# Interaction-network tower on one core: outer sums as float32 products in two row halves, features spread through DRAM, layer-1 rows turned in their own bank

## The chip, the cores and the metric

One core of one Trainium2 chip runs the kernel. The metric is device time in microseconds for one execution, as the median of several. The engines are TensorE (PE: matmuls, and PEld for its weight loads), VectorE (DVE), ScalarE (ACT), GpSimd (POOL, which here only issues gathers) and SyncE (SP, which issues the other DMAs). SBUF is the memory of 128 partitions on which all engines work. PSUM, eight banks of 512 float32 columns in each partition, is where matmuls put their results. A semaphore wait holds up everything behind it on its engine.

## The reference, cut to what matters

512 rows, each with 39 features of 16 numbers looked up in 39 tables, go through two layers of a compressed interaction network and then through an ordinary three-layer perceptron:

```python
B, M0, D = 512, 39, 16
e = stack([tbl_f[ids[:, f]] for f in range(39)], axis=1)        # [B, 39, 16]
X0 = Xi = e
for W in (W0, W1):                                              # [39*39, 128], [39*128, 128]
    z = einsum('bmd,bnd->bdmn', X0, Xi).reshape(B, D, -1)
    Xi = einsum('bdp,po->bod', z, W)                            # [B, 128, 16]
    res.append(Xi)
z = sum(concatenate(res, axis=1), axis=-1)                      # [B, 256]
h = concatenate([z, dense_ctx], axis=1)                         # [B, 272]
h = relu(h @ W_top1 + b_top1); h = relu(h @ W_top2 + b_top2); y = h @ W_top3
```

The sum over `d` at the end lets the second layer be computed without its own pairwise products: for each row of the batch the kernel forms G = X1 (128 x 16) times X0 (16 x 39), and multiplies G by W1. These G are called the outer sums here.

## The kernel before, in words

**Tiles, chunks, steps.** The batch is cut into 4 tiles of 128 rows, each tile into 4 chunks of 32 rows. A chunk has 512 columns (32 rows times 16 of d). Layer 1 of a chunk takes PT = 7 steps: in each one, 128 products of feature pairs (DVE, L738) are multiplied with a piece of W0 and summed in a bank. So there are 16 chunks, STEPS = 112 steps and SPT = 28 steps in a tile. Every engine has the same loop over the steps `s` written out, with the work of other stages put at fixed offsets: `chunk_at(s, offset)` gives the chunk whose step 0 was `offset` steps ago. Which engine is how far ahead is decided only by the semaphores.

**Layer 1.** For chunk i, PE multiplies the features `xs` with 0/1 matrices `sel`. This gives two factors a and b, which ACT copies to `factors` (L433), and three selections, which stay in `b_bank`. DVE multiplies a factor with a selection into `z` (L738). ACT rounds `z` to `z_hi` (float32r, L537), DVE takes the remainder `z_lo` (L748), and PE, LAG = 5 steps later, adds three float32r matmuls of 512 columns to `l1_bank[i % 2]` (L943 to L945, for the last step of a chunk one, L941). In tile 0 two steps of a chunk do without the split: one float32 matmul on `z` kept whole, L938.

**From layer 1 to the outer sums.** ACT copies the bank to `xi` (L553, step 11 of the chunk). PE turns `xi` in four transposes into `xi_bank` (L952, step 13). ACT rounds it to `xit_hi` (L559, step 13), and DVE takes the remainder `xit_lo` out of the same bank (`rest_xit`, L755, step 15). The other side of the product is `diag`: for eight rows of the batch, 8 x 16 partitions against 8 x 40 columns, nonzero only where both belong to the same row (the 40th column is a one, for the sum over d). It is filled from factor a: PE turns its first 40 rows in four transposes into `turn_bank` (`turn_a`, L908, step 1), ACT rounds (`take_xt`, L440), DVE takes the remainder (`rest_xt`, L762), and SP spreads `xt` over `diag` in eight DMAs (L394) for each chunk, high and low parts together. The outer sums of eight rows are then three float32r matmuls of 320 columns (`g_block`, L967 to L969). Four such blocks stand at steps 17, 19, 21 and 23 of the chunk, and ACT copies each to `g` (L545) before the next may start, since there is one `g_bank`.

**Layer 2** of a tile is 39 float32 products of 128 columns (L982) into `s2_bank`, spread over the steps of the next tile; for the last tile they stand together at the end. The perceptron for the first three tiles runs in the last steps, and for the last tile at the very end.

**Features.** Gathers (POOL) and lookups fill `feat`. ACT and DVE split it into three bf16 parts, in pieces (`groups`, three to a tile), and PE turns the parts of the next tile in two halves (`turn_x`, L878), which ACT copies to `xs` (L422).

**Banks.** `turn_bank` takes in turn the features' first half, factor a and the turned factor. `xi_bank` takes the features' second half, factor b and the turned `xi`. `turn_free` makes PE wait until what stood in the bank has been taken.

**SP** issues, in this order: the inputs, then for each chunk the eight diagonals, and behind those of chunks 0 to 2 one piece of w1 each, behind those of chunk 3 the perceptron's weights.

## Time and profile before

| | |
|---|---|
| time, median of 3 runs | 270.82 us (270.24 to 270.98) |
| span of the profiled execution | 273.8 us |
| PE busy | 236.8 us, 86% |
| PEld busy | 185.0 us, 68% |
| DVE busy | 195.6 us, 71% |
| ACT busy | 172.6 us, 63% |
| POOL busy | 104.8 us, 38% |
| DMA queue of SP | 27736 packets, 9.09 MB |

The span runs from the first to the last instruction of one profiled execution. The profile's table by slices shows the granted TensorE clock; full speed is 2.4 GHz and the other level is 1.2 GHz. Shares of the whole span hide that the stages differ, so the rows below are by stretch. In a row of the timeline the first number is the start, the second the duration of the row (or of several of one kind, merged), and a matmul's duration includes the draining of its results. Idle time stands in brackets with what ended it.

### The profile page before, as it was taken

The numbers are of one execution on the slowest core, as the hardware profiler recorded it, in microseconds if no ns is written. First come the engines' busy times: TensorE is split into PE (matmuls) and PEld (weight loads), VectorE is DVE, ScalarE is ACT, GpSimd is POOL, SyncE is SP. The second block draws the span as 40 slices with busy tenths as digits, with TensorE's granted clock in tenths as the row PEclk, the third lists the DMA queues.
The fourth block names the chain that finished last, engine by engine and source line by source line (L and its number), as shares of the span: only waits on it lengthen the run. The fifth ranks groups of instructions, "written<-read, shape, count | busy, mean of one in ns | idle before, by whom it ended". The sixth has DMA issues, their size and how long they took to land.

```text
span 273.8 us, 5185 instructions
## 1 busy us (share of the span) xinstructions
PE 236.8 (86%) x1821; PEld 185.0 (68%) x1821; DVE 195.6 (71%) x341; ACT 172.6 (63%) x339; POOL 104.8 (38%) x102
## 2 busy tenths in 40 slices
PE   4686967896975988787989979988999999999997
PEld 4584954443553655555678768776878788988895
DVE  1453985799994588998978699997889978424001
ACT  4674483267584667776796887869677674457202
POOL 4767876425672565686555548300000000000000
PEclk9959595899996899999999999999999999999999
DMA  6900000006420153412021110201011010010000
GB/s 162 229 11 7 6 8 7 4 15 150 93 61 5 25 141 101 101 13 27 8 35 32 28 23 12 29 2 24 11 15 21 12 19 10 16 24 0 2 0 0
DMA packets 30897, 10.21 MB, mean 37 GB/s; under 512 B 21032, under 2 KB 30269, under 8 KB 30872
## 3 DMA queue, kind: packets, MB, share of 16 engines
q1 hardware_dynamic: 27736, 9.09, 15.2%
q0 software_dynamic: 3136, 0.81, 3.3%
q8 instruction: 14, 0.23, 0.3%
q14 instruction: 11, 0.09, 0.1%
HBM read 7.26 MB, written 0.00 MB: 27 GB/s over the span
## 4 chain that ended last, share of the span: by engine, by line
PE 67%; DVE 10%; issue 10%; ACT 8%; another core or an unknown queue 3%; DMA 1%; DVEq 0%; SPq 0%; ACTq 0%
PE s_bank L982 12%; PE l_bank L945 6%; PE l_bank L943 5%; PE l_bank L944 5%; DVE z L738 4%; PE g_bank L967 3%; PE g_bank L968 3%; PE g_bank L969 3%; PE l_bank L857 3%; PE b_bank L857 3%; DVE z_lo L748 2%; PE b_bank L923 2%; PE xi_bank L952 2%; ACT z_hi L537 2%
## 5 line engine op out<-in xcount | busy, mean ns | idle before, releaser
L363 POOL DMA_INDIRECT feat<-tbl,ids_sb x98 | 104.6, 1068 | 68.8 <-PE l_bank L945 30.6
L738 DVE TENSOR_TENSOR z<-factors,b_bank 128x512 f32<-128x512 f32 x96 | 65.0, 681 | 11.4 <-PE l_bank L938 4.0
L537 ACT ACTIVATE z_hi<-z 128x512 fp32r<-128x512 f32 x104 | 65.8, 633 | 11.0 <-DVE z L738 7.6
L748 DVE TENSOR_TENSOR z_lo<-z,z_hi 128x512 fp32r<-128x512 f32 x88 | 60.3, 685 | 3.6 <-ACT z_hi L537 2.7
L982 PE MATMUL s_bank<-g,w_sb 128*128 128x128 f32 x312 | 46.1, 277 | 0.0
L982 PEld LDWEIGHTS s_bank<-g,w_sb 128*128 128x128 f32 x312 | 41.8, 190 | 1.8 <-issue 0.7
L545 ACT ACTIVATE g<-g_bank 128x320 f32<-128x320 f32 x64 | 27.9, 435 | 23.7 <-PE g_bank L969 15.8
L943 PE MATMUL l_bank<-z_hi,w_hi 128*128 128x512 f32 x88 | 42.6, 484 | 0.0
L967 PE MATMUL g_bank<-diag,xit_hi 128*128 128x320 f32 x64 | 28.5, 446 | 8.5 <-issue 5.8
L945 PE MATMUL l_bank<-z_hi,w_lo 128*128 128x512 f32 x88 | 35.0, 397 | 0.0
L944 PE MATMUL l_bank<-z_lo,w_hi 128*128 128x512 f32 x88 | 34.8, 395 | 0.0
L967 PEld LDWEIGHTS g_bank<-diag,xit_hi 128*128 128x128 f32 x64 | 12.7, 199 | 15.6 <-issue 10.7
L923 PE MATMUL b_bank<-xs,sel 117*128 117x512 bf16 x48 | 18.9, 394 | 2.3 <-DVE z L738 1.1
L968 PE MATMUL g_bank<-diag,xit_hi 128*128 128x320 f32 x64 | 20.0, 312 | 0.0
L969 PE MATMUL g_bank<-diag,xit_lo 128*128 128x320 f32 x64 | 19.9, 310 | 0.0
L945 PEld LDWEIGHTS l_bank<-z_hi,w_lo 128*128 128x128 f32 x88 | 16.7, 189 | 3.8
L943 PEld LDWEIGHTS l_bank<-z_hi,w_hi 128*128 128x128 f32 x88 | 17.0, 193 | 1.2 <-issue 0.7
L944 PEld LDWEIGHTS l_bank<-z_lo,w_hi 128*128 128x128 f32 x88 | 16.9, 192 | 0.4
L923 PEld LDWEIGHTS b_bank<-xs,sel 117*128 117x128 bf16 x48 | 4.7, 98 | 15.7 <-issue 9.0
L553 ACT ACTIVATE xi<-l_bank 128x512 f32<-128x512 f32 x16 | 9.6, 597 | 6.8 <-PE l_bank L941 3.9
L568 ACT ACTIVATE g<-b_bank,bt_sb 128x384 f32<-128x384 f32 (+1 forms) x8 | 3.7, 473 | 15.8 <-PE b_bank L1023 11.0
L968 PEld LDWEIGHTS g_bank<-diag,xit_hi 128*128 128x128 f32 x64 | 12.3, 193 | 1.6 <-issue 0.4
(197 smaller groups left out, 405.6 us busy)
## 6 DMA issues: line engine op xcount, KB each, us to landing
diag<-xt SPq DMA_DIRECT2D x128, 20.0 KB
w_sb<-w SPq DMA_DIRECT2D x3, 832.0 KB
feat<-tbl,ids_sb POOLq DMA_INDIRECT x98
wt_sb<-wt SPq DMA_DIRECT2D x2, 512.0 KB
g<-small SPq DMA_DIRECT2D x1, 770.0 KB
g<-small SPq DMA_DIRECT2D x1, 448.0 KB
w0p<-w_pair SPq DMA_DIRECT2D x1, 448.0 KB
w0m<-w_mirror SPq DMA_DIRECT2D x1, 448.0 KB
```

The costliest lines, as they stand in the source:

```text
L363: nc.gpsimd.indirect_dma_start(feat[:, bt % 2, n * D:(n + 1) * D], None, tables[order[n]], bass.IndirectOffsetOnAxis(ids_sb[:, bt, order[n ...
L537: nc.scalar.activation(z_hi[:, s % RING, :], z[:, at, :], ACT.Copy).then_inc(rounded, 1)
L738: nc.vector.tensor_tensor(target, one, other, ALU.mult).then_inc(product, 1)
L748: nc.vector.tensor_sub(low[rows, s % RING, :], z[rows, SPLITS[s] % Z_RING, :], z_hi[rows, s % RING, :].bitcast(f32)).then_inc(remainder, 1)
L923: nc.tensor.matmul(b_bank[q % B_RING][:], sel[:, j, :], columns(*divmod(i, CPT)), start=True, stop=True).then_inc(selected, 1)
L943: nc.tensor.matmul(bank[:], w0_hi[:, t, :], z_hi[:, t, :], start=u == 0, stop=False)
L944: nc.tensor.matmul(bank[:], w0_hi[:, t, :], z_lo[:, t, :], start=False, stop=False)
L945: nc.tensor.matmul(bank[:], w0_lo[:, t, :], z_hi[:, t, :], start=False, stop=False).then_inc(l1_used, 1)
L967: nc.tensor.matmul(o, y_hi, x_hi, start=True, stop=False)
L968: nc.tensor.matmul(o, y_hi, x_lo, start=False, stop=False)
L969: nc.tensor.matmul(o, y_lo, x_hi, start=False, stop=True).then_inc(g_summed, 1)
L982: last = nc.tensor.matmul(s2_bank[:, 0:P], w1_sb[:, order[m], :], g[:, bt % 2, m, :], start=m == 0, stop=m == F - 1)
```

## The change

**Outer sums.** A block is no longer three float32r matmuls but one product in float32, with no rounding and no remainder. Eight rows of the batch are cut in two halves of four (HB = 4): partitions 0 to 63 and 64 to 127 are two matmuls of 64 rows and 160 columns, the upper half into one bank, the lower into another. `g_bank` is now two banks. Two blocks make a group (GS = 2), a chunk has two groups (GPC = 2), at steps 15 and 18, and ACT copies both banks of a group in one instruction. The order of the batch's rows in `g` differs for it, and `dense_ctx` and `y` are permuted to match.

**Layer-1 rows.** `xi` is turned into `l1_bank[i % 2]`, the bank that it came from, and ACT copies it whole (`take_xit`); `rest_xit` is gone. Layer 1 of chunk i waits for the copy of chunk i - 2.

**Diagonals.** `turn_a`, `take_xt` and `rest_xt` are gone. ACT copies each piece of the features, as float32 and ordered by d, to `line` (`keep_line`). Once per tile SP writes `line` to a DRAM scratch `lines`, waits for it, and reads it back in eight DMAs of 16 x 16 runs of 160 bytes into `diag`, which now holds a whole tile. The loop of SP is paced by layer 1 (`l1_used`).

**Banks.** With `xi_bank` gone, `turn_bank` takes features, factor a and factor b. `w0m` borrows the place of `xit`, and the products kept whole have a tensor of their own.

**Steps.** Layer 2 of a tile starts at step 40 and not 45 of it; for tile 2 it is spread over 16 steps and not 12. The perceptron's first part starts at the same step, 117.

```diff
-G_AT = [TURN_XI + 4 + 2 * r for r in range(CH // P)]
-TURN_A = 1
-REST_XT = TURN_A + 1
+G_AT = [TURN_XI + 2, TURN_XI + 5]
+GPC = len(G_AT)
+GS = SUBS // GPC
+HB = SB // 2
...
+LINE_AT = [[1, 2, 3], [10, 16, 21], [11, 18, 24], [11, 18, 24]]
...
-S2_STEPS = [SPT - 2] * (TILES - 2) + [12]
+S2_STEPS = [SPT - 2] * (TILES - 2) + [16]
...
-        xit_hi = sb("xit_hi", [P, 2, CH], f32r)
-        xit_lo = sb("xit_lo", [P, 2, CH], f32r)
-        xt = sb("xt", [P, 2, 2, SUBS, GW], f32r)
-        diag = sb("diag", [P, 2, 2, SUBS, SB, GW], f32r)
+        xit = sb("xit", [P, 2, CH])
...
+        line = sb("line", [P, 2, D, GW])
+        diag = sb("diag", [P, 2, CPT * SUBS, HB, GW])
...
-        xi_bank = bank("xi_bank")
-        g_bank = bank("g_bank")
+        g_bank = ctx.enter_context(nc.psum_tensor("g_bank", [P, 2, 512], f32))
+        g_banks = [g_bank[:, h, :] for h in range(2)]
...
                 if bt >= 2:
                     pool.wait_ge(*after(turn_filled, "x", bt - 2, XJ - 1))
+                    pool.wait_ge(lined, line_pieces[bt - 1])
...
+            def spread_lines(bt):
+
+                sp.wait_ge(lined, line_pieces[bt + 1])
+                sp.dma_start(lines[bt], line[:, bt % 2, :, :]).then_inc(line_out[bt], 16)
+                sp.wait_ge(line_out[bt], 16)
+                if bt >= 2:
+                    sp.wait_ge(g_summed, CPT * GPC * (bt - 1))
+                for b in range(SB):
+                    sp.dma_start(diag[b * D:(b + 1) * D, bt % 2, :, b % HB, :],
+                                 lines[bt, b::SB].rearrange("r d m -> d r m")).then_inc(diag_in[bt % 2], 16)
...
             for i in range(CHUNKS):
-                sp.wait_ge(*after(turn_taken, "xt", i, 0))
-                if i >= 2:
-                    sp.wait_ge(g_summed, SUBS * (i - 1))
-                for b in range(SB):
-                    sp.dma_start(diag[b * D:(b + 1) * D, i % 2, :, :, b, :].bitcast(f32),
-                                 xt[b * D:(b + 1) * D, i % 2, :, :, :].bitcast(f32)).then_inc(diag_in[i % 2], 16)
+                if i:
+                    sp.wait_ge(l1_used, PT * (i - 1) + 1)
+                if i % CPT == 0:
+                    spread_lines(i // CPT)
...
-            def take_xt(i):
+            def keep_line(bt, k):
+
+                lo, hi = groups[bt][k]
+                if bt >= 2:
+                    act.wait_ge(line_out[bt - 2], 16)
+                act.wait_ge(rest1, split_no[bt, k] + 1)
+                nc.scalar.activation(line[:, bt % 2, :, lo:hi],
+                                     feat[:, bt % 2, lo * D:hi * D].rearrange("p (m d) -> p d m", d=D),
+                                     ACT.Copy).then_inc(lined, 1)
...
-            def round_xit(i):
-                act.wait_ge(*after(turn_filled, "xi", i, 0))
+            def take_xit(i):
+                act.wait_ge(xi_turned, i + 1)
                 if i >= 2:
-                    act.wait_ge(g_summed, SUBS * (i - 1))
-                nc.scalar.activation(xit_hi[:, i % 2, :], xi_bank[:], ACT.Copy).then_inc(xit_hi_done, 1)
+                    act.wait_ge(g_summed, GPC * (i - 1))
+                nc.scalar.activation(xit[:, i % 2, :], l1_bank[i % 2][:], ACT.Copy).then_inc(xit_copied, 1)
...
-            def rest_xit(i):
-            def rest_xt(i):
-            def turn_a(i):
...
             def g_block(j):
...
+                for q in range(GS):
+                    r = n * GS + q
+                    for h in range(2):
+                        rows = slice(h * P // 2, (h + 1) * P // 2)
+                        last = nc.tensor.matmul(g_banks[h][:, q * HB * GW:(q + 1) * HB * GW],
+                                                xit[rows, i % 2, r * P:(r + 1) * P],
+                                                diag[rows, bt % 2, c * SUBS + r, :, :].rearrange("p b m -> p (b m)"),
+                                                start=True, stop=True)
+                last.then_inc(g_summed, 1)
```

On PE, in a chunk of tile 1 (layer 2 of tile 0 runs beside it), from a selection over one block of outer sums to the turn of factor a, this stood before:

```order
L923 MATMUL b_bank0<-xs,sel 128x512 [waits product]
L967 MATMUL g_bank<-diag,xit_hi 128x320 [waits g_copied]
L968 MATMUL g_bank<-diag,xit_hi 128x320
L969 MATMUL g_bank<-diag,xit_lo 128x320
L982 MATMUL s2_bank<-g,w1_sb 128x128
L943 MATMUL l1_bank0<-z_hi,w0_hi 128x512 [waits remainder]
L944 MATMUL l1_bank0<-z_lo,w0_hi 128x512
L945 MATMUL l1_bank0<-z_hi,w0_lo 128x512
L908 MATMUL turn_bank<-id32,factors 128x40 [waits turn_taken0]
L908 MATMUL turn_bank<-id32,factors 128x40 x3
L982 MATMUL s2_bank<-g,w1_sb 128x128 x2
```

and this now, at the first group of a chunk:

```order
L914 MATMUL b_bank0<-xs,sel 128x512 [waits product]
L978 MATMUL s2_bank<-g,w1_sb 128x128 x2
L934 MATMUL l1_bank0<-z_hi,w0_hi 128x512 [waits remainder]
L935 MATMUL l1_bank0<-z_lo,w0_hi 128x512
L936 MATMUL l1_bank0<-z_hi,w0_lo 128x512
L961 MATMUL g_bank<-diag,xit 128x160 [waits g_copied,xit_copied]
L961 MATMUL g_bank<-diag,xit 128x160 x3
L978 MATMUL s2_bank<-g,w1_sb 128x128
```

Two blocks of three became one group of four, and the turn of factor a (L908) is gone.

On PE, where the features of the next tile are turned in two halves, before (`parts` is what the features were split into; `turn_taken0` is counted when the content of `turn_bank` was taken, `turn_taken1` for `xi_bank`):

```order
L878 MATMUL turn_bank<-id16,parts 117x128 [waits kept,rest2,turn_taken0]
L878 MATMUL turn_bank<-id16,parts 117x128 x7
L967 MATMUL g_bank<-diag,xit_hi 128x320 [waits g_copied]
L968 MATMUL g_bank<-diag,xit_hi 128x320
L969 MATMUL g_bank<-diag,xit_lo 128x320
L982 MATMUL s2_bank<-g,w1_sb 128x128
L943 MATMUL l1_bank0<-z_hi,w0_hi 128x512 [waits remainder]
L944 MATMUL l1_bank0<-z_lo,w0_hi 128x512
L945 MATMUL l1_bank0<-z_hi,w0_lo 128x512
L878 MATMUL xi_bank<-id16,parts 117x128 [waits turn_taken1]
L878 MATMUL xi_bank<-id16,parts 117x128 x7
```

and now:

```order
L879 MATMUL turn_bank<-id16,parts 117x128 [waits kept,rest2,turn_taken0]
L879 MATMUL turn_bank<-id16,parts 117x128 x7
L978 MATMUL s2_bank<-g,w1_sb 128x128 x2
L934 MATMUL l1_bank0<-z_hi,w0_hi 128x512 [waits remainder]
L935 MATMUL l1_bank0<-z_lo,w0_hi 128x512
L936 MATMUL l1_bank0<-z_hi,w0_lo 128x512
L879 MATMUL turn_bank<-id16,parts 117x128 [waits turn_taken0]
L879 MATMUL turn_bank<-id16,parts 117x128 x7
```

The second half waits for the copy of the first, with no outer sums between them.

On DVE, around the last step of a chunk in tile 1, before:

```order
L738 TENSOR_TENSOR z<-factors,b_bank1 128x512 [waits turn_taken1,selected,rounded,remainder]
L748 TENSOR_TENSOR z_hi<-z,z_hi 39x512 [waits l1_used,rounded]
L755 TENSOR_TENSOR xit_lo<-xi_bank,xit_hi 128x512 [waits g_summed,xit_hi_done]
L646 TENSOR_TENSOR rest<-feat 128x128 [waits kept,rest2,gathered2_2]
L738 TENSOR_TENSOR z<-factors,b_bank0 128x512 [waits selected,rounded,remainder]
L748 TENSOR_TENSOR z_lo<-z,z_hi 128x512 [waits l1_used,rounded]
L762 TENSOR_TENSOR xt<-turn_bank,xt 128x4x39 [waits diag_in1,xt_hi_done]
L653 TENSOR_TENSOR parts<-rest 128x16x8 [waits turn_filled1,rest1]
```

and now:

```order
L756 TENSOR_TENSOR z<-factors,b_bank1 128x512 [waits turn_taken0,selected,rounded,remainder]
L766 TENSOR_TENSOR z_hi<-z,z_hi 39x512 [waits l1_used,rounded]
L667 TENSOR_TENSOR rest<-feat 128x128 [waits kept,rest2,gathered2_2]
L756 TENSOR_TENSOR z<-factors,b_bank0 128x512 [waits selected,rounded,remainder]
L766 TENSOR_TENSOR z_lo<-z,z_hi 128x512 [waits l1_used,rounded]
L674 TENSOR_TENSOR parts<-rest 128x16x8 [waits turn_filled0,rest1]
```

The two remainders L755 and L762 are gone; the rest stands in the same order.

## Rows read from the trace of the kernel before

**Rows 1.** Windows by stage: from:to, us, then busy us of PE, PEld, DVE, ACT, POOL; clock.

```profile
54.00:76.00 22.00, 18.57 (x77) 9.44 (x77) 21.58 (x39) 14.07 (x28) 10.23 (x11) 1.00 0.41 90
76.00:95.00 19.00, 14.49 (x68) 9.56 (x67) 12.14 (x23) 11.72 (x24) 9.92 (x11) 0.82 0.12 18
95.00:128.00 33.00, 27.57 (x137) 18.74 (x137) 30.15 (x53) 23.83 (x52) 21.95 (x21) 1.00 0.36 81
128.00:156.00 28.00, 25.61 (x165) 20.38 (x164) 22.79 (x39) 21.30 (x44) 15.72 (x16) 1.00 0.16 25
156.00:184.00 28.00, 25.62 (x157) 20.07 (x156) 27.20 (x51) 22.28 (x48) 12.08 (x12) 1.00 0.12 16
184.00:258.00 74.00, 72.38 (x445) 60.62 (x443) 51.00 (x87) 48.97 (x99) 0.00 (x0) 1.00 0.09 14
```

**Rows 2.** Windows 54:76, 95:128, 156:184, summed: L755 alone, then L762 alone.

```profile
sum 83.00, DVE 4.84; mean DVE 1.61
...
sum 83.00, DVE 2.83; mean DVE 0.94
```

**Rows 3.** Timeline of DVE: start, duration, engine, line, operation.

```profile
194.17 0.32 DVE L762 TENSOR_TENSOR xt<-turn_bank,xt 128x156 fp32r<-128x156 f32 x1 [0.72 <-ACT xt L440]
194.41 0.68 DVE L738 TENSOR_TENSOR z<-factors,b_bank 128x512 f32<-128x512 f32 x1
195.00 0.69 DVE L748 TENSOR_TENSOR z_lo<-z,z_hi 128x512 fp32r<-128x512 f32 x1
```

**Rows 4.** Timeline of PE, one block of outer sums and what follows it.

```profile
196.56 0.31 PE L967 MATMUL g_bank<-diag,xit_hi 128*128 128x320 f32 x1
...
197.00 0.27 PE L982 MATMUL s_bank<-g,w_sb 128*128 128x128 f32 x1
```

**Rows 5.** Windows with L967 alone: PE busy and count, one for each block.

```profile
128.00:156.00 28.00, 4.09 (x9) 1.77 (x9) 1.00 0.16 25
184.00:258.00 74.00, 11.42 (x28) 5.42 (x28) 1.00 0.09 14
```

**Rows 6.** Windows with L908 alone: PE busy and count, four for each turn.

```profile
128.00:156.00 28.00, 0.88 (x8) 0.64 (x8) 1.00 0.16 25
184.00:258.00 74.00, 1.75 (x16) 1.29 (x16) 1.00 0.09 14
```

**Rows 7.** Timeline of PE around one turn of factor a (L908).

```profile
193.03 0.40 PE L945 MATMUL l_bank<-z_hi,w_lo 128*128 128x512 f32 x1
193.36 0.44 PE L908 MATMUL turn_bank<-id,factors 40*128 40x40 f32 x4
193.73 0.49 PE L982 MATMUL s_bank<-g,w_sb 128*128 128x128 f32 x2
...
194.29 0.39 PE L944 MATMUL l_bank<-z_lo,w_hi 128*128 128x512 f32 x1
194.52 0.40 PE L945 MATMUL l_bank<-z_hi,w_lo 128*128 128x512 f32 x1
```

**Rows 8.** Lines of PE from 258.2 to 266.8: count, busy us, mean ns.

```profile
L982 PE MATMUL s_bank<-g,w_sb 128*128 128x128 f32 x78 | 9.0, 276 | 0.0
```

**Rows 9.** Timeline of PE, the two turns of tile 3's features.

```profile
182.37 0.63 PE L878 MATMUL turn_bank<-id,parts 128*117 128x128 bf16 x8 [0.72 <-DVE parts L653]
...
184.25 0.44 PE L878 MATMUL xi_bank<-id,parts 128*117 128x128 bf16 x5
```

**Rows 10.** Timeline of ACT, the copy of the first half.

```profile
183.86 1.02 ACT L422 ACTIVATE xs<-turn_bank 117x1024 bf16<-117x1024 bf16 x1
```

**Rows 11.** Timeline of SP: the first chunk's eight diagonals, issue time.

```profile
57.60 5.24 SPq L394 DMA_DIRECT2D diag<-xt  x8
```

**Rows 12.** Timeline of PE, the first block of outer sums of the program.

```profile
73.58 0.41 PE L967 MATMUL g_bank<-diag,xit_hi 128*128 128x320 f32 x1
```

**Rows 13.** Waits: who waited, releaser, total us, times, longest us.

```profile
ACT g L545 <- remote: 6.0, 3, 2.9
```

**Rows 14.** DMA issues: KB, us from issue to landing.

```profile
ids_sb<-ids SPq DMA_DIRECT2D x1, 78.0 KB, 1.9
```

More of the change, by code:

```diff
@@ L284, in build @@
         chunk0_taken = sem("chunk0_taken")
-        xt_hi_done = sem("xt_hi_done")
+        lined = sem("lined")
+        line_out = [sem(f"line_out{j}") for j in range(TILES)]
         w0_summed = sem("w0_summed")
@@ L318, in build @@
         fills = [[("x", 0, 0)], [("x", 0, 1)], [("a", 0, 0)], [("b", 0, 0)]]
-        for s in range(LAST):
+        for s in range(STEPS):
             bt, v = divmod(s, SPT)
-            if (i := chunk_at(s, TURN_A)) is not None:
-                fills[0].append(("xt", i, 0))
             if bt + 1 < TILES:
@@ L342, in after, with turn_bank_of @@
             return sems[k], n + 1
+        def turn_bank_of(*job):
+            return turn_banks[fill[job][0]]
+        line_pieces = [sum(len(groups[b]) for b in range(t)) for t in range(TILES + 1)]
         MLP_MM = H1T + H2T + 1
@@ L423, in take_x @@
                     xs[:, bt % 2, first:end, k * D // XJ:(k + 1) * D // XJ],
-                    turn_banks[k][0:R, :].bitcast(bf16).rearrange("p (d b) -> p b d", b=P)[:, first:end, :],
-                    ACT.Copy).then_inc(signal or turn_taken[k], 1)
+                    turn_bank_of("x", bt, k)[0:R, :].bitcast(bf16).rearrange("p (d b) -> p b d", b=P)[:, first:end, :],
+                    ACT.Copy).then_inc(signal or turn_taken[fill["x", bt, k][0]], 1)
             def take_factor(name, i):
@@ L588, in _ @@
                             keep_next(bt + 1, k)
+                for t in (bt, bt + 1):
+                    for k, at in enumerate(LINE_AT[t] if t < TILES else ()):
+                        if v == at and (t == 0 or t == bt + 1):
+                            keep_line(t, k)
                 if s == TOP_AT[0]:
@@ L591, in _ @@
                     nc.scalar.activation(wt1_hi[:], wt1_sb[:], ACT.Copy).then_inc(top_rounded, 1)
-                for j, (at, part) in enumerate(zip(ZS_AT, whole)):
+                for j, (at, part) in enumerate(zip(ZS_AT, (z1, z2))):
                     if s == at:
@@ L791, in _ @@
                     rest_z(s - Z_LAG)
-                if (i := chunk_at(s, REST_XI)) is not None:
-                    rest_xit(i)
-                if (i := chunk_at(s, REST_XT)) is not None:
-                    rest_xt(i)
                 if bt + 1 < TILES:
@@ L899, in fill_factor @@
                 k = fill[name, i, 0][0]
-                nc.tensor.matmul(turn_banks[k][:], sel[:, SELECTS + "ab".index(name), :], columns(i // CPT, i % CPT),
+                nc.tensor.matmul(turn_banks[k], sel[:, SELECTS + "ab".index(name), :], columns(i // CPT, i % CPT),
                                  start=True, stop=True).then_inc(turn_filled[k], 1)
-            def turn_a(i):
-                turn_free("xt", i, 0)
-                pe.wait_ge(*after(turn_taken, "a", i, 0))
-                for r in range(SUBS):
-                    last = nc.tensor.transpose(turn_bank[:, r * GW:(r + 1) * GW],
-                                               factors[0:GW, i % F_RING, 0, r * P:(r + 1) * P],
-                                               id32[0:GW, 0:GW])
-                last.then_inc(turn_filled[fill["xt", i, 0][0]], 1)
             def select(i, j):
```

135 lines of the change are left out of this document (57 added, 78 removed).

## The prediction

> **What bounds the kernel now.** Read the table by stretches first [rows 1]. Its columns give, for each stretch, how long each engine was busy. What to look for is which engine fills the stretch. The work stages begin at 54 us, when the first product of tile 0 starts. VectorE (DVE) fills 21.58 of 22 us, then 30.15 of 33 us (95 to 128) and 27.20 of 28 us (156 to 184). TensorE (PE) fills 72.38 of the 74 us from 184 to 258, and in 128 to 156 it is ahead of DVE, 25.61 to 22.79. In 76 to 95 neither is full: that stretch has a halt and a lower granted clock, 0.82 of full. So a microsecond taken from DVE counts in three stretches (83 us), one taken from PE in two others (102 us).
>
> Then read starts, not durations. A row's duration on PE contains the time in which results drain while the next matmul already streams. The float32r product L967 lasts 0.31 us, but its row and the next two start 0.15 us apart, and the row behind the three starts 0.44 us after the first [rows 4]. 0.44 us is what one block of outer sums costs PE. On DVE the rows last 0.68 but start 0.60 apart, and the small L762 takes 0.24 [rows 3].
>
> **Part 1: the remainders leave DVE.** Each chunk loses `rest_xit` (L755, 0.60) and `rest_xt` (L762, 0.24). In the three stretches where DVE is full the sums of their busy time are 4.84 and 2.83 us; divided by 0.69 and 0.31 us a row (0.32 in [rows 3] is one such row) that is 7 and 9 instructions [rows 2]. 7 x 0.60 + 9 x 0.24 = 6.4 us less on DVE. What is late next is PE: it is busy 18.57, 27.57 and 25.62 us there, with draining in it. In the first two it leaves room. In 156 to 184 the gap between DVE and PE is only 1.6 us (27.20 less 25.62) where DVE loses 2.5, so I take 1.5 there. Part 1: 5.4 us gained, between 4.4 (if PE soon catches up in the second too) and 6.4.
>
> **Part 2: the outer sums on PE.** Before: 64 blocks of three float32r matmuls of 320 columns. After: 32 groups, each of two column ranges by two row halves, written as four float32 matmuls of 160 columns. A float32 matmul is issued as two instructions: the program asks for 39 products of layer 2 in a tile, and the last tile shows 78 rows of L982, back to back [rows 8]. 9.0 us for 78, less one drain of 0.16, is 0.114 us for 128 columns; 160 columns cost in proportion 0.14. A group is thus 8 instructions of 0.14.
>
> Two things decide its price. First, the array changes from full height to halves and back for each group. The nearest row is the old turn of the factors (L908, 40 rows, tile of 64): from L945 at 193.03 to L944 at 194.29 is 1.26 us, in which stand L945 (0.23, as L944 to L945 one step on), two L982 (0.11 each) and L943 (0.23); 0.58 is left for four tiny transposes [rows 7]. They start some 0.07 apart (0.44 us busy in all, of which the last is 0.235), so 0.27 is their own and 0.31 is entering and leaving the mode. Second, whether the two halves run at the same time. If they do not, the group is 0.31 + 8 x 0.14 = 1.43 us. If they do, the second instruction of the upper half can run beside the first of the lower one, but a half still runs its own two in order; in this order of issue the eight take five slots: 0.31 + 5 x 0.14 = 1.01 us. No row of before shows two halves at once. I take 1.01, since the halves share neither rows of the array, nor weights, nor a bank (h goes to its own bank), and the turn's rows show that the array does treat a 64-row tile as a mode of its own. Both ends stay for the range.
>
> By the Trainium skill (TensorE: Matmul & The Clock Gate, Part 3: Packing small matmuls), matmuls at different row positions run concurrently, starting about 4 ns apart, while matmuls otherwise stay in program order; with full pairing a group would be 0.31 + 4 x 0.14 = 0.87 us and my sum 2.6 us lower. No run here shows that yet.
>
> In the two stretches that PE fills there are 9 + 28 blocks [rows 5] and 8 + 16 transposes, six turns [rows 6]. Before: 37 x 0.44 + 6 x 0.58 = 19.8 us. After, 18.5 groups: 18.7 us overlapped (1.1 gained), 26.5 us one after another (6.7 lost). So the precision change by itself brings PE little; the removed turns pay for the mode changes.
>
> **Part 3: one bank for five kinds of fills.** The factors a and b and both halves of the features now go through `turn_bank`. Fill a, a step after fill b, waits for ScalarE's (ACT's) copy of b; behind it on PE stand layer 1's matmuls of that step. Where DVE paces, PE has that slack. Where PE paces, a step lasts 1.5 us (L945 to L945 in [rows 7]), and ACT's copy of 512 columns, shorter than the 1.02 us of the features' copy of 1024 [rows 10], fits in it: cost 0. Without that cover (ACT late with its other work) it is up to 0.5 us for each of 12 chunks. The second half of the features has no such room: the first turn starts at 182.37, the second at 184.25 [rows 9], and ACT's copy in between takes 1.02 us [rows 10]. Now the second waits for the end of that copy. With the outer sums no longer between them PE would arrive about 0.4 us early: 0.4 x 3 tiles = 1.2 us lost (0 to 3).
>
> **Part 4: features by way of DRAM.** 128 small transfers become 4 writes and 32 reads, and w1 queues behind 9 of them and not behind 8. ACT trades 16 `take_xt` for 12 `keep_line`, and half of its `take_g` rows for rows of twice the size; it is never the full engine [rows 1], so 0. The first tile alone is tight. The lines are complete after step 3, about 60 us; a write lands in some 2 us (ids_sb took 1.9 [rows 14]); the eight reads are issued in 5.2 us, as the eight diagonals were [rows 11]; they land 2 us later, at 69. The first outer sums stood at 73.58 [rows 12] and now are due two steps sooner, at about 71. Cover 2 us: cost 0, up to 4 if the landing is late. Later tiles have 15 steps of cover.
>
> **Part 5: looser coupling.** `take_g` once in 3 or 4 steps and not in 2, and one copy fewer between turn and outer sum. PE's gaps in the stretches it fills sum to 2.4 + 1.6 us [rows 1]; I take 0.7 of it.
>
> **Sum.** -5.4 - 1.1 + 1.2 + 0 - 0.7 = -6.0 us. The profiled execution has a span of 273.8 us, 3.0 above the median of 270.82; I carry the difference over unscaled: 270.82 - 6.0 = 264.8 us, with 261 to 268 for this case. All bounds here are inside: 4.4 instead of 5.4, 3 instead of 1.2.
>
> **Rivals.**
> A. The halves run one after another. Part 2 becomes +6.7, and in 156 to 184 PE's own growth leaves 1.0 of the 2.5. Part 1 is then 4.9: -4.9 + 6.7 + 1.2 = +3.0, so 273.8 us, slower. It decides at the group's price: above 1.35 us a group (halfway and more to 1.43) the gain of part 1 is eaten. For it: no row shows an overlap, and each float32 product has two ordered instructions. Against it: separate rows, weights and banks.
> B. The first reads land late. The w1 pieces and gathers share the queues with them, and PE waits at the first group: +3 to +4 on the forecast, 268.5 us. For it: 2 us of cover only, two trips in a row. Against it: w1 is now issued behind the reads, where before it went between the first diagonals.
> C. The early halts go. ACT stood three times, 6.0 us in all, before L545, released by nothing that the profile knows [rows 13], and the stretch from 76 to 95 has them and the low clock [rows 1]. If they come from transfers among the w1 pieces, the other order may end some of them: -5 more, 259.5 us. Against it: nothing names their cause.
> That the change does not do what it says is A.
>
> **How the numbers follow.** Forecast 0.50, A 0.20, B 0.15, C 0.15. A is the only case that ends above 271.6; B and the upper edge of the forecast leave some 0.08 within 0.3% (about 0.8 us, what a measurement here can tell from no change). Faster 0.72, same 0.08, slower 0.20. The range 258.0 to 273.5 holds the forecast, B, most of C and the nearer third of A.
>
> **What would show it.** DVE: no rows of L755 and L762, and DVE no longer full in 95 to 128. PE: start to start of the four products of a group, 0.14 within a half, and from the first to the row behind the group, 0.85 (overlapped, less the entry) or 1.25. PE idle before the second turn of a tile's features about 0.4 us. The first outer sum at 71 to 72 us, with diag landed. Wrong would be: a group at 1.4 us or more; PE waiting for ACT's factor copies in every chunk; the first group later than 73.6.

## The result, and the profile after

On the chip of the prediction the changed kernel takes 262.92 us in the median of four runs (260.08 to 266.09), against 270.9 before. The ratio, here and below, leaves out executions more than 1.5% above the fastest of their kernel (here 264.5 and 266.1 us): it is 0.962, with a 95% interval from 0.954 to 0.970. The forecast was 264.8 us, and the range 258.0 to 273.5.

The experiments ran later, on chips with the numbers 0, 2, 8 and 15; the number of the first chip is not recorded. On those four the kernel before takes 252.9 to 253.3 us, and on chip 0, beside the changed kernel, 253.1 against 244.7, a ratio of 0.966 (0.962 to 0.970). Of the 23.0 us between the two profiles of the kernel before (273.8 and 250.8), 13.2 lie ahead of the part that is studied here: the first product stands at 53.9 us on the first chip and at 40.7 us on chip 0. The other 9.8 lie in chunks 0 to 9.

The stages of the changed kernel, as [rows 1], by the same columns. The stretches stand where its own stages stand:

```profile
52.20:76.00 23.80, 17.18 (x76) 9.33 (x76) 22.19 (x38) 17.21 (x33) 10.67 (x12) 1.00 0.60 140
76.00:95.00 19.00, 15.02 (x86) 9.26 (x87) 14.11 (x24) 14.09 (x27) 12.89 (x13) 1.00 0.37 88
95.00:128.00 33.00, 28.62 (x172) 19.33 (x171) 29.69 (x52) 26.29 (x50) 21.96 (x23) 1.00 0.13 18
128.00:156.00 28.00, 25.32 (x168) 18.39 (x166) 23.54 (x40) 23.64 (x41) 17.50 (x18) 1.00 0.17 29
156.00:184.00 28.00, 27.62 (x187) 20.57 (x185) 24.46 (x43) 23.11 (x44) 5.11 (x5) 1.00 0.09 21
184.00:246.00 62.00, 61.22 (x396) 48.02 (x396) 37.83 (x63) 37.00 (x65) 0.00 (x0) 1.00 0.02 4
```

Two things changed against [rows 1]. The stretch 76 to 95 has the full clock (it had 0.82). And in 156 to 184 the full engine is now PE (27.62 of 28 us) and no longer DVE (24.46, it was 27.20). In 95 to 128 DVE is still nearly full, at 29.69 of 33 (it was 30.15), with 22 products of L756 where there were 21 of L738. In 76 to 95 neither engine is full, as before.

One group of outer sums, in the timeline of PE (start, duration, then what ran), with its neighbours:

```profile
191.34 0.39 PE L935 MATMUL l_bank<-z_lo,w_hi 128*128 128x512 f32 x1
191.56 0.40 PE L936 MATMUL l_bank<-z_hi,w_lo 128*128 128x512 f32 x1
191.89 0.81 PE L961 MATMUL g_bank<-diag,xit 64*128 64x160 f32 x8
192.63 0.49 PE L978 MATMUL s_bank<-g,w_sb 128*128 128x128 f32 x2
```

And the same group in very short windows, with L961 alone (the number behind x counts the matmul rows that are running in the window):

```profile
191.88:191.90 0.02, 0.01 (x2) 0.01 (x2) 1.00 0.00 0
...
192.12:192.14 0.02, 0.02 (x4) 0.02 (x4) 1.00 0.00 0
...
192.26:192.28 0.02, 0.02 (x6) 0.02 (x4) 1.00 0.00 0
```

Within 20 ns two rows start, and later two more within 20 ns, and so on: the eight instructions run as four pairs. The starts are 191.890 and 191.896, then 192.13, 192.27 and 192.40, each with a partner 6 ns later. L936 has streamed for its 0.22 us by 191.79; the group starts 0.1 later, its first pair takes 0.24 and the others 0.135, and of the 0.21 between the two L978 behind it 0.1 is more than their usual 0.11. In all a group costs PE 0.95 us: 4 x 0.135 = 0.54, and 0.41 beyond it, which I put down to entering and leaving the mode.

The price of the shared bank, in the list of waits (who waited, for whom; us in total, times, longest us):

```profile
DVE z L756 <- ACT factors L447: 10.7, 8, 2.2
...
PE turn_bank L901 <- ACT factors L447: 7.5, 5, 3.2
```

Before, DVE's wait for the same copy was 3.8 us, six times, and PE had no such wait among its longer ones. The first group, and SP's issues ahead of it:

```profile
70.67 0.81 PE L961 MATMUL g_bank<-diag,xit 64*128 64x160 f32 x8
```

```profile
57.12 0.35 SPq L395 DMA_DIRECT2D lines<-line  x1
59.30 4.04 SPq L400 DMA_DIRECT2D diag<-lines  x8
63.39 5.53 SPq L419 DMA_DIRECT2D w_sb<-w  x3
```

It stands at 70.67 us, 2.9 us earlier than the first block in [rows 12], and PE did not wait for `diag` there. Of the 2.9 us, 1.7 lie ahead of chunk 0, which starts at 52.2 us and not at 53.9.

The halts of [rows 13] are there again, though shorter: where ACT stood 6.0 us in three, the list of waits of the changed kernel on this chip has

```profile
ACT g L564 <- remote: 3.2, 2, 2.5
```

and more of the kind before other copies of ACT.

### The profile page after: what moved, and what is told of

Its sections match the earlier page's. It is cut to its first block, busy times and chain, and to the rows that moved or that the text cites. A ratio compares the mean times of both kernels' runs of the same rounds, so it can differ in the third digit from the quotient of the medians.

```text
span 258.2 us, 4953 instructions
## 1 busy us (share of the span) xinstructions
PE 220.1 (85%) x1821; PEld 163.4 (63%) x1821; DVE 182.5 (71%) x308; ACT 171.8 (67%) x303; POOL 103.1 (40%) x102
## 4 chain that ended last, share of the span: by engine, by line
PE 69%; ACT 10%; issue 9%; DVE 7%; another core or an unknown queue 2%; DMA 1%; SPq 0%; ACTq 0%; DVEq 0%
PE s_bank L978 15%; PE g_bank L961 7%; PE l_bank L936 7%; PE l_bank L934 7%; PE l_bank L935 6%; ACT z_hi L555 3%; PE b_bank L914 3%; PE l_bank L942 2%; PE turn_bank L901 2%; PE g_bank L858 2%; PE s_bank L858 2%; PE turn_bank L879 2%; PE l_bank L858 2%; PE l_bank L1043 2%
## 5 line engine op out<-in xcount | busy, mean ns | idle before, releaser
L368 POOL DMA_INDIRECT feat<-tbl,ids_sb x98 | 102.9, 1050 | 61.2 <-PE l_bank L936 26.3
L756 DVE TENSOR_TENSOR z<-factors,b_bank 128x512 f32<-128x512 f32 x88 | 60.3, 685 | 16.4 <-ACT factors L447 10.7
L555 ACT ACTIVATE z_hi<-z 128x512 fp32r<-128x512 f32 x104 | 63.6, 631 | 7.6 <-PE l_bank L936 2.7
L978 PE MATMUL s_bank<-g,w_sb 128*128 128x128 f32 x312 | 48.5, 282 | 2.4 <-ACT g L564 1.3
L978 PEld LDWEIGHTS s_bank<-g,w_sb 128*128 128x128 f32 x312 | 43.0, 192 | 8.4 <-issue 5.1
L564 ACT ACTIVATE g<-g_bank 128x640 f32<-128x640 f32 x32 | 22.5, 702 | 21.0 <-PE g_bank L961 17.4
L936 PE MATMUL l_bank<-z_hi,w_lo 128*128 128x512 f32 x88 | 34.9, 396 | 0.0
L961 PE MATMUL g_bank<-diag,xit 64*128 64x160 f32 x256 | 26.1, 322 | 3.5 <-ACT xit L578 2.8
L961 PEld LDWEIGHTS g_bank<-diag,xit 64*128 64x128 f32 x256 | 18.3, 186 | 14.9 <-issue 9.3
L447 ACT ACTIVATE factors<-turn_bank 128x512 f32<-128x512 f32 x30 | 17.9, 596 | 6.2 <-PE turn_bank L901 3.5
L936 PEld LDWEIGHTS l_bank<-z_hi,w_lo 128*128 128x128 f32 x88 | 16.5, 188 | 3.7
L901 PE MATMUL turn_bank<-xs,sel 117*128 117x512 bf16 x30 | 11.6, 386 | 7.5 <-ACT factors L447 7.5
L578 ACT ACTIVATE xit<-l_bank 128x512 f32<-128x512 f32 x16 | 9.6, 598 | 3.3 <-remote 3.3
```

The source lines that it names most:

```text
L368: nc.gpsimd.indirect_dma_start(feat[:, bt % 2, n * D:(n + 1) * D], None, tables[order[n]], bass.IndirectOffsetOnAxis(ids_sb[:, bt, order[n ...
L447: nc.scalar.activation(factors[:, i % F_RING, "ab".index(name), :], turn_banks[k], ACT.Copy).then_inc(turn_taken[k], 1)
L555: nc.scalar.activation(z_hi[:, s % RING, :], z[:, at, :], ACT.Copy).then_inc(rounded, 1)
L564: nc.scalar.activation(to.rearrange("p m (k q) -> p m k q", k=2), g_bank[:, :, 0:GS * HB * GW].rearrange("p k (q m) -> p m k q", m=GW), AC ...
L756: nc.vector.tensor_tensor(target, one, other, ALU.mult).then_inc(product, 1)
L936: nc.tensor.matmul(bank[:], w0_lo[:, t, :], z_hi[:, t, :], start=False, stop=False).then_inc(l1_used, 1)
```

## The experiments

Ratios are to the kernel before, in the same comparison on the same chip. Chip 8 had the halves in turn, the products twice and both runs on the remainders; chip 0 the two kernels again and both runs on the fills; chip 2 the later layer 2, the three moves and the bridge; chip 15 the moves and lines. Differences between two kernels are those of their ratios, at 253.1 us, also where the two ran on different chips. The **changed kernel again**, and the **kernel before, profiled again**:

> The changed kernel itself, beside the kernel before on the same chip, since in the last comparison the kernel before took 253.3 us and not 270.8. If the change is worth a fixed share: a ratio of 0.962 to the kernel before. If a part of the gain was the halts and the low clock around 85 us that the kernel before had on the first chip: 0.965 to 0.975. The version with the halves one after another in the program had 0.9655; since both halves ran at once there too, I expect the same here within 0.3%.

Measured: 244.7 us in the median of six, ratio 0.966 (0.962 to 0.970). Four of them lie between 242.6 us, at a mean granted clock of 0.986, and 245.0, at 0.965; the other two took 249.2 and 249.8, at 0.952.

> The kernel before, profiled on this chip. If the halts (all engines idle at about 75, 84 and 115 us) belong to the kernel, they are there again, and the span is that of the table of before. If they belong to the chip or to the one execution, there are none, and the span is some 251 us.

Measured: 252.6 us, span 250.8, and no halt: no wait of ACT before L545 from outside the profile's knowledge, as [rows 13] had, and the clock full from 47 us on. Nor does the list of waits of the next experiment, the changed kernel with another order of the halves, while on the first chip both kernels have them. So the halts come with the first chip or with those executions, and not with the kernel. Since the change is worth the same share, within the intervals, where there are none, they are not where its gain comes from either. What caused them stays open. The profiles on the later chips give a table free of halts; the changed kernel stands in it by the next experiment, whose time is the same. The numbers are spans, in us, between the starts of the first product (L738, L756) of chunks 0, 10 and 15, from the timelines of DVE:

| profile | ahead of chunk 0 | chunks 0 to 9 | 10 to 14 | 15 to the end | span |
|---|---|---|---|---|---|
| kernel before | 40.7 | 102.9 | 55.7 | 51.5 | 250.8 |
| before, without remainders | 40.9 | 98.4 | 54.4 | 51.9 | 245.6 |
| changed (halves in turn) | 41.5 | 99.6 | 54.0 | 47.5 | 242.6 |
| changed, remainders back | 41.2 | 104.7 | 56.7 | 47.5 | 250.1 |
| changed, products twice | 40.9 | 106.3 | 59.5 | 50.3 | 257.0 |
| changed, three moves | 41.1 | 97.2 | 52.2 | 48.4 | 238.8 |

**The order of the halves.**

```diff
-                for q in range(GS):
-                    r = n * GS + q
-                    for h in range(2):
+                for h in range(2):
+                    for q in range(GS):
+                        r = n * GS + q
```

> The changed kernel, but a group's four float32 products in the order upper half twice, then lower half twice, and not alternating. Theory (matmuls start in program order and only neighbours of different halves overlap): of the eight instructions only the fourth and the fifth pair up, so a group takes 7 slots of 0.135 and not 4, +0.4 us for each of 32 groups, 13 of them beside a full VectorE: +0.4 x 19 to +0.4 x 32 = +8 to +13 us on the changed kernel's 260 to 261. Rival (each half has a queue of its own, so the order in the program does not matter): no change, 260 to 261. Rival (PE's price for the group is not what the time hangs on): the trace shows 7 slots, the time moves by less than 3 us.

Measured: 245.1 us, ratio 0.966 (0.959 to 0.972), as the changed kernel. The timeline of PE, and the short windows with L961 alone:

```profile
165.61 0.40 PE L936 MATMUL l_bank<-z_hi,w_lo 128*128 128x512 f32 x1
165.94 0.82 PE L961 MATMUL g_bank<-diag,xit 64*128 64x160 f32 x8
166.69 0.38 PE L978 MATMUL s_bank<-g,w_sb 128*128 128x128 f32 x1
```

```profile
165.93:165.96 0.03, 0.02 (x2) 0.02 (x2) 1.00 0.00 0
...
166.17:166.20 0.03, 0.03 (x4) 0.03 (x4) 1.00 0.00 0
```

My theory fell. The program gives the upper half's four instructions first, then the lower half's four, and still they run in pairs. Only the partner comes 13 ns later and not 6. From the first start to the last it is 0.525 us in all 32 groups, against 0.518.

The rows don't name their half. A rival would be that the two instructions of one product are the pair; the new order would not have touched that. Two readings speak against it. Those two stand next to each other in both programs, yet the distance to the partner doubled, as did the number of instructions from an upper one to its lower one (two, now four). And at full height the two instructions of a product start 0.11 us apart and not together (78 rows in 9.0 us, [rows 8]). By this, matmuls on two halves of the rows do not wait for each other's turn.

**The products twice.**

```diff
-                    for h in range(2):
+                    for h in (0, 1, 0, 1):
```

> The changed kernel, but each group of outer sums is multiplied twice over (the same values written again), so 8 paired slots of 0.135 and not 4: +0.54 us for each of 32 groups, 17.3 us of PE's time in all. If PE is what the time hangs on only in the two stretches that it fills (18.5 groups): +10 us. If it paces everywhere now that VectorE has lost its remainders: +17 us. If VectorE still paces most of it: +5 us or less.

Measured: 258.8 us, ratio 1.021 (1.016 to 1.025), 13.9 us above the changed kernel. PE got 32 x 0.54 = 17.3 us more, and 0.8 of it arrives in the time. From the starts of L756, chunks 3 to 14 are 0.8 to 1.2 us longer each, where two groups are 1.08; only chunks 5 and 9 are not. So added PE time counts in nearly the whole kernel, and not in two stretches only.

**The remainders put back** on DVE, with a tensor of their own in place of the real ones:

```diff
+                for at, w in ((TURN_XI + 2, CH), (2, SUBS * F)):
+                    if (i := chunk_at(s, at)) is not None:
...
+                        nc.vector.tensor_sub(spare[:, 0:w], spare[:, 0:w], spare[:, 0:w]).then_inc(spare_done, 1)
```

> The changed kernel, with one VectorE subtraction of 512 columns (0.6 us) and one of 156 columns (0.24 us) put back into each chunk at the steps where the old kernel had the remainders; their results are not used. Theory (part 1 of the prediction is worth about 5 us): +3 to +6 us on 260 to 261. Rival (PE paces the new kernel everywhere, and VectorE has room): under +1.5 us.

Measured: 252.6 us, ratio 0.999 (0.996 to 1.002), +8.4 us on the changed kernel, above what either theory had. The windows show where the excess arises (columns as in [rows 1]):

```profile
92.00:96.00 4.00, 1.29 (x11) 0.50 (x7) 4.00 (x8) 3.40 (x7) 3.39 (x3) 0.95 0.08 6
96.00:99.00 3.00, 2.18 (x7) 1.81 (x8) 2.84 (x6) 2.69 (x6) 2.38 (x2) 0.50 0.03 3
99.00:102.00 3.00, 3.00 (x12) 2.38 (x11) 2.94 (x5) 1.17 (x3) 1.83 (x1) 0.50 0.19 38
```

From 92 to 96 us PE was busy 1.29 of 4 us; then its granted clock stood at half, the 1.2 GHz level, until 102. Chunk 6 lasted 13.0 us, against 10.4 in the changed kernel, and the same came again in chunk 10 (12.9 against 10.3). Those two chunks make 5.2 of the 8.4 us. Chunks 4 and 5, at the full clock, grew by 0.8 us each, the subtractions' own 0.84; so some 1.8 us of each 2.6 come with the waits and the low clock, an estimate.

**The kernel before without its remainders**: both subtractions left out, the third product of a block reads the rounded rows again, the low half of `diag` is zero.

```diff
-                if (i := chunk_at(s, REST_XI)) is not None:
-                    rest_xit(i)
-                if (i := chunk_at(s, REST_XT)) is not None:
-                    rest_xt(i)
```

> The kernel before, with VectorE's two remainders of each chunk left out (the low part of the features' diagonal is zero, and the third product of an outer sum reads the rounded rows again, so PE, ACT and the transfers do the same work as before). Theory (part 1 by itself is worth 5.4 us, 4.4 to 6.4): 264.4 to 266.4. If the gain of the change hangs on both (VectorE and PE so close that the one alone gives little): 268 to 270. If leaving the remainders out also takes away the early halts: 260 to 263.

Measured: 247.5 us, ratio 0.976 (0.972 to 0.980), -6.0 us. Its outer sums are not those of the reference, since the low parts are missing; PE, ACT and the transfers do the work of before. This is part 1 of the prediction by itself. By the table 4.5 of it comes in chunks 0 to 9 and 1.3 in 10 to 14.

**The fills of the shared bank**, first apart (FILL_B = 2 and the line copies elsewhere), then ACT's factor copies ahead of its other work:

> The changed kernel with fill b one step earlier, so that two steps and not one lie between the fills of b and a, and with the copies of the features' lines moved to steps in which ACT copies no factor. Theory (VectorE waits 10.7 us for the factors' copies, since both fills share one bank): a ratio 0.5 to 1.5% below that of the changed kernel, and VectorE's wait for the factors under 6 us. Rival (those waits are VectorE waiting in another place for the same PE): no change of the time, the wait for factors shorter, and another wait longer.

> The changed kernel with ACT's copies of the two factors directly behind the rounding of the step, ahead of its other copies (lines, feature parts, outer sums, layer 1). Theory (the factor's copy is late because ACT has other work ahead of it): 0.3 to 1% below the changed kernel. Rival (ACT then waits for PE's fill, which stands late in PE's step, and the copies of outer sums and of layer 1 behind it come late): 0 to 2% above.

Measured: 243.9 us, ratio 0.962 (0.957 to 0.968), not to be told from the changed kernel, with DVE's wait for the factors at 9.1 us and not under 6; and 250.0 us, ratio 0.988 (0.984 to 0.992), 5.6 us worse. In the second, ACT's wait in the list of waits is the rival's:

```profile
ACT factors L447 <- PE turn_bank L901: 11.2, 14, 1.4
```

It was 4.1 us in six waits. The copy was not late for its place alone; PE's fill is late too, and everything of ACT's behind it waits along. DVE's wait for the factors fell to 6.9 us, without gain.

**Layer 2 two steps later**, and **three moves**:

```diff
-S2_AT = SPT - PT + G_AT[-1] + 1
+S2_AT = SPT - PT + G_AT[-1] + 3
-S2_STEPS = [SPT - 2] * (TILES - 2) + [16]
+S2_STEPS = [SPT - 2] * (TILES - 2) + [14]
```

```diff
-FILL_B = 3
+FILL_B = 2
-EMBED_AT = [8, SPT + 2]
+EMBED_AT = [12, SPT + 5]
-LINE_AT = [[1, 2, 3], [10, 16, 21], [11, 18, 24], [11, 18, 24]]
+LINE_AT = [[1, 2, 3], [10, 17, 21], [12, 19, 24], [12, 19, 24]]
```

The first diff alone is layer2_later; three_moves has both.

> The changed kernel with layer 2 of tiles 0 to 2 starting two steps later (three steps behind the tile's last group of outer sums, not one; the third tile's share is then spread over 14 steps and not 16). Theory (PE stands 1.2 to 1.3 us at steps 40 and 68 since layer 2 follows right on a group that ACT has still to copy, and after it the granted clock falls to half in some executions, which costs up to 2.9 us in chunk 6): those two waits go, no low clock at 95 or 143 us, ratio to the kernel before 0.955 to 0.962 against 0.966. Rival (VectorE is full there and PE only waits elsewhere): the wait shows at the next instruction that needs VectorE, ratio 0.965 to 0.968.

> The changed kernel with three things moved: fill b one step earlier, so that ACT has a step more to empty the shared bank before fill a; ACT's embedding copies of tiles 2 and 3 and its line copies in steps without a factor copy; layer 2 two steps later as in layer2_later. Nothing is added or left out. Theory (the shared bank's 3.2 us wait at chunk 2 and the two waits before layer 2 are schedule faults, not the price of the change): chunks 1 and 2 together 1 to 3 us shorter, ratio 0.950 to 0.958. Rival (VectorE's full stretches set the time there, and the waits are only room): ratio as layer2_later.

Measured: 242.0 us, ratio 0.956 (0.952 to 0.960); and 240.5 us, ratio 0.950 (0.948 to 0.953). The ratios are those of the two theories, at their lower edges. The profile of layer2_later has the full clock at 95 and 143 us, and PE's wait of 1.2 us for the group's copy went; but 0.9 us of it stands again at the turn of `xi` behind it. In three_moves chunks 1 and 2 take 18.5 us together, against 19.4, just under the 1 to 3 us that I expected. Three moves beats both kernels: 12.6 us under the one before, 3.9 under the changed one, with nothing added. A wait that shrank is in PE's timeline. In the changed kernel (halves in turn), with idle time and its releaser in brackets:

```profile
52.64 0.40 PE L936 MATMUL l_bank<-z_hi,w_lo 128*128 128x512 f32 x1
56.21 0.61 PE L901 MATMUL turn_bank<-xs,sel 117*128 117x512 bf16 x1 [3.17 <-ACT factors L447]
```

The same place with three moves:

```profile
51.61 0.40 PE L936 MATMUL l_bank<-z_hi,w_lo 128*128 128x512 f32 x1
53.76 0.39 PE L901 MATMUL turn_bank<-xs,sel 117*128 117x512 bf16 x1 [1.75 <-ACT factors L447]
```

Why the first is so long, ACT's timeline of the changed kernel shows:

```profile
52.71 0.94 ACT L507 ACTIVATE parts<-rest 128x416 bf16<-128x416 bf16 x1
54.23 0.63 ACT L555 ACTIVATE z_hi<-z 128x512 fp32r<-128x512 f32 x1 [0.58 <-DVE z L756]
54.77 0.91 ACT L456 ACTIVATE line<-feat 128x416 f32<-128x416 f32 x1
55.57 0.59 ACT L447 ACTIVATE factors<-turn_bank 128x512 f32<-128x512 f32 x1
```

Factor b lies in the bank from 52.3 us (L901 at 51.95, 0.38 long). ACT works on parts, the rounding and the new line copy first, and fill a on PE, with all of layer 1 behind it, stands until the copy has run.

**Bridged**: unread products in front of five of PE's longer waits (the one of 1.7 us at step 4 has none).

```diff
+BRIDGE = {11: 7, 39: 4, 40: 4, 67: 4, 68: 4}
...
+                if s in BRIDGE:
+                    c = -(-(s - LAG) // PT)
...
+                    for _ in range(BRIDGE[s]):
+                        nc.tensor.matmul(l1_bank[c % 2][:], sel[:, 0, :], sel[:, 0:4, :].rearrange("p q c -> p (q c)"),
+                                         start=True, stop=True)
```

> The changed kernel with 23 products that nobody reads (128 columns of weights by 512, 0.22 us each, into the free bank of layer 1) put in front of the five places at which PE stands longest: 7 at step 11, 4 each at steps 39, 40, 67 and 68. PE's work grows by 5 us, all meant to fall into its own waits. Theory (what those waits cost is the granted clock that falls after them): no clock under 1.0 from 95 us on in any execution, the ratio at the lower edge of the changed kernel's, 0.958 to 0.962, and less spread between executions. Rival (the clock has nothing to do with those waits): the low stretches stay, and the ratio is 0.966 to 0.975.

Measured: 242.0 us, ratio 0.957 (0.954 to 0.959). Five microseconds of useless work on the engine that mostly sets the time made the kernel 2.4 us faster, just past my theory's 0.958 to 0.962. The windows with a low clock: first the changed kernel (halves in turn), then remainders_back, then the same three windows of bridged (columns as in [rows 1]):

```profile
50.00:60.00 10.00, 6.83 (x24) 4.02 (x23) 8.57 (x15) 7.03 (x12) 6.60 (x7) 0.83 0.90 203
```

```profile
90.00:100.00 10.00, 6.47 (x31) 4.55 (x30) 9.84 (x18) 7.52 (x14) 8.02 (x7) 0.78 0.06 5
135.00:145.00 10.00, 6.85 (x42) 4.39 (x41) 9.51 (x17) 8.38 (x14) 6.50 (x7) 0.92 0.07 5
```

```profile
50.00:60.00 10.00, 8.32 (x40) 4.59 (x40) 8.97 (x16) 7.39 (x15) 7.01 (x8) 1.00 0.95 218
90.00:100.00 10.00, 9.36 (x57) 6.00 (x54) 9.78 (x18) 8.59 (x16) 8.41 (x6) 1.00 0.13 25
135.00:145.00 10.00, 9.47 (x55) 6.29 (x54) 9.94 (x20) 8.62 (x17) 5.52 (x6) 1.00 0.06 6
```

All four executions of bridged have the mean clock 0.986 and lie within 0.7 us. The changed kernel's have 0.986 to 0.965 and spread over 2.4 us. So part of the changed kernel's time, and its scatter, goes with a low clock that follows on PE's waits. The two profiles differ by 2.2 us, and 0.9 of that lies ahead of chunk 0, where the kernels are the same; what bridging itself gave in this pair is about 1.3 us. By the Trainium skill (TensorE: Matmul & The Clock Gate, Part 1: The HAM clock gate), the default state is throttled and activity releases it. The trace agrees: in 50 to 60 us the clock is 0.83 with PE busy 6.83 of 10, and 1.00 with it busy 8.32. But remainders_back had 1.00 in that window with PE busy 6.63, so whether the clock falls differs between executions.

**Moves and lines**: three moves, with the first tile's line copies in steps 1, 3 and 5, and four unread products at step 11.

> three_moves with two more things: the first tile's line copies in steps 1, 3 and 5 and not 1, 2 and 3 (off the steps in which ACT copies the factors), and four unread products of 512 columns ahead of the wait at step 11. The lines leave for DRAM two steps, some 2.5 us, later; the first outer sum stood at 58.4 us in three_moves. Theory (the DRAM route has more cover than my prediction's 2 us, and the small waits at steps 4 and 11 still count): the first outer sum stands within 0.5 us of its old place, PE's wait at step 4 goes, ratio 0.945 to 0.950 against 0.9503. Rival (the cover is used up): PE waits for diag at the first outer sum, 1 to 2.5 us, ratio 0.953 to 0.960. Rival (VectorE sets the time of those chunks anyway): ratio 0.949 to 0.952, and nothing waits for diag.

Measured: 243.0 us, ratio 0.962 (0.959 to 0.965), 2.9 us worse than three moves, and by none of my mechanisms. The first group stands at 58.25 us, even a little earlier, so the DRAM route's cover was not used up. What grew is a wait for gathers. First three moves, then this one, in DVE's timeline:

```profile
65.34 0.26 DVE L667 TENSOR_TENSOR rest<-feat 128x96 f32<-128x96 f32 x1 [1.17 <-DMA feat<-tbl,ids_sb]
```

```profile
66.18 0.26 DVE L668 TENSOR_TENSOR rest<-feat 128x96 f32<-128x96 f32 x1 [2.04 <-DMA feat<-tbl,ids_sb]
```

The w1 pieces left SP 1.4 us later, and the gathers of the second tile's last piece landed 0.8 us later. PE's wait for that piece grew from 1.4 to 2.4 us, and the clock then was 0.57 in the mean of 68.5 to 72.5. That w1 and the gathers get into each other's way is what the order of events suggests; no run here separates them.

## Why the prediction was right, and where it was not

The forecast's mechanism was right in the main; A and B fell, and C is at most a small part. A: the halves overlap. B: the first group stands 2.9 us earlier than the first block did. (On the first chip the gathers have POOL's queue, and only w1 SP's with the reads, so that rival had one neighbour less than I gave it.) C: the share of the gain is the same, within the intervals, where there are no halts. On the first chip they were shorter in the changed kernel's profile (3.2 us and not 6.0), and chunks 0 to 9 shrank there by 8.1 us (112.7 to 104.6) against 3.3 on the later chips. The two profiled executions are 15.6 us apart, the kernels 10.2 by the ratio; a small part of those 10.2 may be C's. The measured time is 2 to 4 us below the forecast's 264.8 (262.9 in the median of four, 260.7 by the ratio), at the edge of its own 261 to 268. One sign did not come: DVE is still nearly full in 95 to 128. The steps of the sum:

**Part 1, the remainders leave DVE: -5.4, right.** Alone they are worth 6.0 us in the old kernel, inside 4.4 to 6.4. Put back into the new one they cost 8.4; the excess comes with the low clock in chunks 6 and 10, which the prediction did not have.

**Part 2, the outer sums on PE: -1.1, right in sign and too small.** A group costs 0.95 us and not 1.01. The five slots came from the thought that a half's two instructions hold back the other half's; they don't. What lies beyond the slots costs 0.41 and not 0.31, which takes most of that back. With 0.95 the two stretches give 19.8 - 18.5 x 0.95 = -2.2 us. The larger error is that I let PE count in two stretches alone. Over the whole program the change saves PE 64 x 0.44 + 16 x 0.58 - 32 x 0.95 = 7.0 us, and the doubled products show that 0.8 of added PE time counts once the remainders are gone: some 5.6 us, an estimate, and an upper one, since PE paces less the less it has to do.

On the page named in the prediction (TensorE: Matmul & The Clock Gate, Part 3: Packing small matmuls) the Trainium skill has the pairing right, but it also calls matmuls strictly first in, first out. The run with the halves in turn speaks against that, if the pairs are made across the halves as read above: four instructions of one half stand ahead of the other's four, and each starts 13 ns from a partner. The measurement decides.

**The end, a term that I left out.** From the start of chunk 15 the changed kernel is 4.0 us shorter on the first chip and on the later ones alike (51.5 to 47.5). Layer 2 of tile 2 starts five steps sooner, so that 118 rows of L978 stand behind that point where 138 of L982 did: 20 x 0.11 = 2.2 us, moved ahead into chunks 13 and 14, which are not longer by as much (21.8 us together before, 21.5 after). Six groups in place of 14 blocks are 0.5 us, the turn of factor a is 0.6. The last 0.7 I can't assign.

**Part 3, one bank: the sign was right, the place wrong.** I put the cost on the features' second half (1.2 us for three tiles); PE waited 0.7 us for it, once. The rows allowed more than I took: the copy of [rows 10] ends at 184.88, 0.63 us behind the old start of the second turn, so with PE 0.4 us early a tile would have lost 1.0, not 0.4. I put the factors at nothing, with a bound of 0.5 us a chunk. But DVE's wait for their copies grew from 4.1 to 10.1 us on the later chips, in seven waits of up to 2.2 us. What failed is the step that ACT's copy fits into PE's step at no cost, and that PE has the slack where DVE paces. ACT is never the full engine of a stretch; but in the middle of tile 0's second chunk it had 0.94 + 0.63 + 0.91 us of other copies ahead of this one. The worst wait can cost twice, once as time and once by the clock behind it (0.83 in 50 to 60 us). Moving copies and fills out of each other's way, with layer 2 two steps later, gave 3.9 us back. Of these, 2.6 are layer 2's two steps alone. That wait, on a group that ACT has still to copy, was not in the prediction either.

**Part 4, the DRAM route: 0, right.** A write takes 2.2 us to land, as estimated, and eight reads 4.0 us to issue, where I had 5.2; and even lines that left later did not hold up the first group. SP's order may not be free of effects, though: in moves_and_lines w1 left later, and a gather landed later.

**Part 5, looser coupling: -0.7, not separated.** PE's wait for ACT's copy at the first matmul of an outer sum fell from 5.7 us (seven waits) to 0.4, but part of it came back as the 2.5 us in front of layer 2. No run isolates the looser coupling.

Together, on the later chips: -6.0 for part 1, some -5.6 for PE, and +3.9 for waits and clock that three moves could take back, is -7.7; measured is 253.1 x 0.034 = -8.6. This is an estimate from terms that overlap (layer 2's shift has none of its own), and the agreement shows no more than that none of them is far off. The sum of the prediction, -6.0, had the right size partly by luck: two errors, PE too small and the bank too cheap, partly cancelled.

## What to carry to other kernels

Before a bank or buffer is shared, look for what its emptying engine has queued ahead of the copy at the worst step, not for its slack on average. Work for the bounding engine is counted over the whole kernel, since removing the other bound widens the stretch in which it paces. And where PE waits for one or two microseconds, see what the granted clock does behind the wait: moving the wait, or filling it with unread products, may be worth more than the wait itself.

## What the hardware showed that I had not expected

- Two float32 matmuls on different halves of the rows pair up even when the program gives one half's four instructions first: starts 13 ns apart, 6 ns when they alternate, and the same 0.52 us from the first start to the last. That the pairs are made across the halves is read from those distances.
- A group in half height took PE 0.41 us beyond the 0.54 us of its four slots. The likely reason is entering and leaving the mode; no run takes it apart.
- After 1.29 us of PE work in 4 us the granted clock stood at half for some 7 us, and the same came again in chunk 10 of that execution. Each of the two chunks was 2.6 us longer, 0.8 of it the added subtractions. Executions of one kernel differ in whether it happens. With the waits bridged, all four had the same mean clock, 0.986, against 0.965 to 0.986.
